# A decoder layer's self-attention: projection parts in odd steps, other work in even steps, and a DMA that adds the fourth tile of three quads

## The chip, the core and the metric

The kernel runs on one core of a Trainium2 chip. The metric is the device time of one execution in microseconds (us). A core has TensorE (PE, matmuls; PEld is its weight load), VectorE (DVE), ScalarE (ACT), GpSimd (POOL) and SyncE (SP, which here only issues DMAs). Each runs its own instruction stream, and the streams wait for one another through semaphores.

## What is computed

A decoder layer on x of 2 x 2048 x 512: self-attention of 16 heads, a layer norm of the sum, cross-attention over 77 context rows, a layer norm, a mixture of 8 experts, a layer norm. The change concerns the self-attention alone:

```python
qkv = x @ qkv_w + qkv_b
q, k, v = ...                                   # 16 heads of 32
attn = softmax(einsum('bnhd,bmhd->bhnm', q, k) * scale)
out = einsum('bhnm,bmhd->bnhd', attn, v) @ proj_w + proj_b
```

## The kernel before

A unit is one batch with four heads (their 4 x 32 features fill 128 partitions); there are 8 units. A unit's 2048 queries are cut into four chunks of 512, so there are 32 chunks (g = 0 to 31). A chunk goes over the 2048 keys in 16 steps (kt) of 128 keys. In each step TensorE makes four scores, one per head (line 706, keys x queries, 128 x 512), in three banks in rotation, and ScalarE takes their exponentials (line 472) into one of four tiles of prob, by kt % 4.

The softmax's shift is the row maximum. It is found ahead: between the scores of chunk g TensorE also makes the 64 maximum passes (line 631) of chunk g + 1, four per step and three steps early, so that the passes of chunk g + 2 begin in step 13 (T - EARLY). They go to three banks (mx) in rotation; VectorE reduces each (line 517), and a pass waits for the reduction three passes before it. After step 12 VectorE takes the maxima over the parts (line 522), negates them (line 526) and makes a low part (line 528); TensorE transposes these in step 13 into the bank misc (line 644), VectorE copies them out in step 14 (line 535), and SyncE issues four DMAs that put the rows below the queries (line 318), at the end of its chunk's list. The next chunk's scores wait for them.

In each even step, after the second score, TensorE runs a burst: it multiplies the values with the two tiles before (line 652). Row sums (the softmax's denominators) go through GpSimd: the tiles of a chunk form four quads, and GpSimd adds tiles 1, 2 and 3 of a quad to its sum, two heads at a time (add_step, line 273, six additions per quad). TensorE sums a quad over the keys (line 660) into misc, quads 0 and 1 in step 15, quads 2 and 3 in steps 1 and 2 of the next chunk. ScalarE copies the sums out in step 2 (line 452), VectorE inverts them in four pieces in steps 3 and 4 (line 542), GpSimd multiplies the values' sums by them (divide, line 279) and SyncE stores the result (line 325). ScalarE may write a prob tile again once GpSimd's addition of it is done.

The queries, keys and values of the units are projected in between. A job (OPS, JOBS) is one 512-wide block of q, k or v in four parts, a part being one matmul of 512 columns (q and k, line 623) or four of 128 (v, line 619) into misc. Up to three jobs stand in a chunk, their parts at the steps of PARTS_AT: a step's first of two parts stands after its second score, the last part at the step's end. In the step after a job's last part (LEAVE_AT) VectorE takes it out of misc: for q and k a rounded high part (line 509) and a low part (line 511), for v one addition (line 498). The first part of the next job waits for that. SyncE, which goes through a fixed list by kt, then issues twelve DMAs of 64 KB per q or k job (move_stack, line 245) that stack high and low parts for the scores, and where a block of x has had its last user the load of the next one (line 312, 1 MB). In step 13 TensorE waits for the stacked queries that chunk g + 2 reads (line 743): in the third and fourth chunk of a unit these come from the chunk's own second job. Chunks 28 to 31 belong to the last unit; only two of its jobs are left there.

The lines that set the order of SyncE's and VectorE's lists around the change:

```python
SUMS_AT, DENS_AT, DIVIDE_AT, STORE_AT = 0, 2, (1, 1), 10
INVERT_AT = ((3, 1), (3, 3), (4, 1), (4, 3))
PARTS_AT = ((3, 3, 4, 5), (6, 7, 7, 8), (9, 10, 11, 11))
LEAVE_AT = {(job.chunk, job.place[-1] + 1): i for i, job in enumerate(JOBS) if job.place}
```

Of the kernel before, what the change touches and what calls it, by code (L numbers as in the profile page):

```python
# [13 lines left out]
P = 128  # L14
# [61 lines left out]
def self_attention(nc, z, keep, block, x, xT_dram, qkv_w, qkv_b, attnT_dram, rows_dram):  # L76
# [13 lines left out]
    LEAD = EARLY * PER_STEP  # L90
    MOVES = 3 * HG
# [4 lines left out]
    QUADS, ADDS = T // 4, 6  # L96
# [5 lines left out]
    SUMS_AT, DENS_AT, DIVIDE_AT, STORE_AT = 0, 2, (1, 1), 10  # L102
    INVERT_AT = ((3, 1), (3, 3), (4, 1), (4, 3))
# [8 lines left out]
    PARTS_AT = ((3, 3, 4, 5), (6, 7, 7, 8), (9, 10, 11, 11))  # L112
# [33 lines left out]
    def stacked_by(i):  # L146

        return 16 * sum(MOVES // 2 if other.place is None else MOVES for other in JOBS[:i + 1]
                        if (other.what, other.n) == (JOBS[i].what, JOBS[i].n))

# [61 lines left out]
    quad_ready, den_mm, recip_ready = s.sem("quad_ready"), s.sem("den_mm"), s.sem("recip_ready")  # L212
# [37 lines left out]
    def _(pool):  # L250
# [9 lines left out]
        def add_step(g, i, k):  # L260


            d = g * QUADS + i
            if k == 1:

                after(pool, den_mm, d - QUADS + 1)
            for half in range(2):
                heads = slice(2 * half, 2 * half + 2)
                pool.wait_ge(prob_ready, (g * T + 4 * i + k) * HG + 2 * half + 2)
                if k > 1:  # L270
                    pool.wait_ge(quad_ready, d * ADDS + 2 * (k - 1) - 1 + half)
                so_far = prob[:, 0, heads, :] if k == 1 else quad_sum[:, i, heads, :]
                pool.tensor_tensor(quad_sum[:, i, heads, :], so_far, prob[:, k, heads, :], ALU.add).then_inc(quad_ready, 1)  # L273
# [24 lines left out]
    def _(sp):  # L298
# [50 lines left out]
        for g in range(LAST):  # L349
            for kt in range(T):  # L350
                if kt == STORE_AT and g > 0:
                    store(g - 1)
                    empty_slots(g - 4)
                if (g, kt) not in LEAVE_AT:
                    continue
# [13 lines left out]
            shift_rows(g + 1)  # L369
# [26 lines left out]
    def _(act):  # L396
# [31 lines left out]

        for chunk in range(NQ):
            load_rows(chunk)  # L430
# [23 lines left out]
        def exponentials(g, fill=None):  # L454
            for kt in range(T):
                step = g * T + kt
                for j in range(HG):
# [26 lines left out]
    def _(dve):  # L484
# [5 lines left out]
        def leave_psum(i):  # L490
# [12 lines left out]
            if job.place is not None:  # L503
                before = SPLITS[order - 2]
                if JOBS[before].place is None:
                    stacked_first(dve, JOBS[before].what, JOBS[before].n)
                else:
                    dve.wait_ge(stacked[JOBS[before].what, JOBS[before].n], stacked_by(before))
                dve.tensor_scalar(hilo[:, order % 2, 0, :], bank[:, :], bias, None, ALU.add).then_inc(hi_ready, 1)
# [4 lines left out]
        def reduce_max(n, m):  # L514
            dve.wait_ge(max_mm, n + 1)
            q, j, k = m // (HG * KQ), m // KQ % HG, m % KQ
            dve.reduce_max(part_max[:, q, j, k:k + 1], mx[n % 3][:, :], AX_X).then_inc(max_read, 1)  # L517
# [36 lines left out]
        for m in range(2):  # L554
            reduce_max(NMAX + m, m)
        leave_shift(0)
        for m in range(2, LEAD):
            reduce_max(NMAX + m, m)

        for g in range(LAST):  # L560
            for kt in range(T):
                for i in range(PER_STEP):
                    n = (g + 1) * NMAX + LEAD + kt * PER_STEP + i
                    if n < CHUNKS * NMAX:
                        reduce_max(n, n % NMAX)
                    if i == 0 and kt == T - EARLY + 1 and g + 1 < CHUNKS:
# [3 lines left out]
                    if (kt, i) in INVERT_AT and g > 0:  # L570
                        invert(g - 1, INVERT_AT.index((kt, i)))
# [9 lines left out]
    def _(pe):  # L581
# [11 lines left out]
        def project_part(i, part):  # L593
# [5 lines left out]
            if part == 0:  # L599
# [9 lines left out]
                if not first and JOBS[i - 1].chunk != job.chunk:  # L609
                    if job.chunk > 0:  # L610
                        pe.wait_ge(dens_ready, job.chunk)
                    else:
                        pe.wait_ge(shiftT_ready, 1)
# [13 lines left out]
        def max_pass(n, m, g):  # L627

            after(pe, max_read, n - 2)
            q, j, k = m // (HG * KQ), m // KQ % HG, m % KQ  # L630
            pe.matmul(mx[n % 3][:, :], q_stack[g % Q_SLOTS][0:QK, j, q * P:(q + 1) * P], k_stack[g // NQ % 2][0:QK, j, k * BANK:(k + 1) * BANK],  # L631
                      start=True, stop=True).then_inc(max_mm, 1)

        def transpose_shift(g):

            pe.wait_ge(shift_ready, g + 1)
            before = [i for (chunk, kt), i in LEAVE_AT.items() if chunk == g - 1]
            if g > 1:
                pe.wait_ge(dens_ready, g - 1)
            if before:  # L640
                i = before[-1]
                pe.wait_ge(v_ready if JOBS[i].what == "v" else hilo_ready, left_psum(i))
            for q in range(TQ):
                last = pe.transpose(misc[0:2 * HG, q * P:(q + 1) * P],
# [11 lines left out]
        def row_sums(d):  # L656

            pe.wait_ge(quad_ready, (d + 1) * ADDS)
# [26 lines left out]
        def burst(g, kt):  # L685
# [12 lines left out]
            for i in OWN_SUMS_AT.get(kt, ()):  # L698
                if i == 0:
                    pe.wait_ge(shiftT_ready, g + 2)  # L700
# [27 lines left out]
        for m in range(LEAD):  # L728
            if m == 2:
# [5 lines left out]
        def chunk(g):  # L735
            pe.wait_ge(shift_in, (g + 1) * 16 * HG)
            for kt in range(T):
# [7 lines left out]
                for i in range(HG):  # L745
                    n = (g + 1) * NMAX + LEAD + kt * PER_STEP + i
                    if n < CHUNKS * NMAX:
# [1459 lines left out]
```

## Time and profile before

| | |
|---|---|
| runs, median (lowest to highest) | 3611.71 us (3609.11 to 3613.97), 3 runs |
| profiled execution, its own time | 3609.78 us |
| its span, first to last instruction | 3608.1 us |
| TensorE busy over the span | 3360.5 us, 93% |
| VectorE busy | 2530.3 us, 70% |
| GpSimd busy | 1996.3 us, 55% |
| ScalarE busy | 1640.8 us, 45% |
| mean granted clock of TensorE | 0.97 |
| stretch of chunks 0 to 31 | about 110 to 2135 us of the span |

The span is one execution on the core; the rest of the execution's time lies around it. Busy shares are of the whole span, of which the self-attention's chunks are the part from about 110 us; the cross-attention and the experts follow. "Granted clock" is TensorE's clock as the records give it, 1.00 being 2.4 GHz and 0.50 being 1.2. Matmuls are pipelined, so that their busy times overlap: where this document prices one, it goes from one start to the next. In the rows, an engine's idle time before an instruction stands in brackets with what ended it.

### The profile page before, as it was taken

The numbers are of one execution on the slowest core, as the hardware profiler recorded it, in microseconds if no ns is written. First come the engines' busy times: TensorE is split into PE (matmuls) and PEld (weight loads), VectorE is DVE, ScalarE is ACT, GpSimd is POOL, SyncE is SP. The second block draws the span as 40 slices with busy tenths as digits, with TensorE's granted clock in tenths as the row PEclk, the third lists the DMA queues.
The fourth block names the chain that finished last, engine by engine and source line by source line (L and its number), as shares of the span: only waits on it lengthen the run. The fifth ranks groups of instructions, "written<-read, shape, count | busy, mean of one in ns | idle before, by whom it ended". The sixth has DMA issues, their size and how long they took to land. (4 is left out here: it accounts for less than half of the span.)

```text
span 3608.1 us, 50073 instructions
## 1 busy us (share of the span) xinstructions
PE 3360.5 (93%) x18021; PEld 2253.7 (62%) x18021; DVE 2530.3 (70%) x4512; ACT 1640.8 (45%) x3043; POOL 1996.3 (55%) x1008
## 2 busy tenths in 40 slices
PE   7999999999999999999999887999859899999996
PEld 5555555555555555554554445887749789898885
DVE  5777777777777777777777745888734765566666
ACT  2455555555555555555555553444312332233332
POOL 2698898998898898898898930011110101110112
PEclk9999999999999999999999988999979999999998
DMA  6312222322313313223220032132132333323332
GB/s 218 111 56 67 71 75 65 94 68 62 110 39 85 87 51 105 55 63 94 62 71 13 16 107 66 56 113 94 47 126 71 131 105 109 110 95 107 127 124 96
DMA packets 190276, 308.47 MB, mean 85 GB/s; under 512 B 25513, under 2 KB 72233, under 8 KB 190010
## 3 DMA queue, kind: packets, MB, share of 16 engines
q1 hardware_dynamic: 166970, 243.82, 22.7%
q0 software_dynamic: 14592, 44.32, 3.6%
q10 hardware_dynamic: 8448, 16.78, 1.3%
q8 instruction: 167, 2.74, 0.3%
q14 instruction: 99, 0.81, 0.1%
HBM read 195.66 MB, written 61.33 MB: 71 GB/s over the span
## 5 line engine op out<-in xcount | busy, mean ns | idle before, releaser
L517 DVE TENSOR_REDUCE sa_part_max<-sa_mx 128x1 f32<-128x512 f32 x2048 | 1288.2, 680 | 487.1 <-PE sa_mx L631 483.8
L472 ACT ACTIVATE sa_prob<-sa_sc 128x512 f32<-128x512 f32 x2017 | 1072.6, 600 | 804.4 <-PE sa_sc L706 755.5
L273 POOL TENSOR_TENSOR sa_quad_sum<-sa_quad_sum,sa_prob 128x1024 f32<-128x1024 f32 x500 | 1175.5, 2381 | 8.1 <-ACT sa_prob L472 7.5
L273 POOL TENSOR_TENSOR sa_quad_sum<-sa_prob 128x1024 f32<-128x1024 f32 x250 | 588.7, 2375 | 225.4 <-ACT sa_prob L472 223.3
L2072 PE MATMUL ex_h<-ex_xT,ex_w 128*128 128x384 f32 (+2 forms) x2688 | 464.0, 328 | 52.2 <-issue 24.1
L631 PE MATMUL sa_mx<-sa_k_even,sa_q_stack 96*128 96x512 f32 x1024 | 492.1, 484 | 9.3 <-DMA sa_q_stack<-sa_shiftT 3.1
L2072 PEld LDWEIGHTS ex_h<-ex_xT,ex_w 128*128 128x128 f32 x2688 | 445.9, 195 | 64.5 <-issue 31.8
L631 PE MATMUL sa_mx<-sa_k_odd,sa_q_stack 96*128 96x512 f32 x1024 | 481.1, 470 | 1.8 <-DVE sa_part_max L517 1.3
L2083 PE MATMUL ex_acc<-ex_w,ex_hT 128*128 128x512 f32 x1719 | 415.6, 392 | 1.5 <-DVE ex_hT L2011 1.3
L706 PE MATMUL sa_sc<-sa_q_stack,sa_k_even 98*128 98x512 f32 x1024 | 407.3, 398 | 0.0
L706 PE MATMUL sa_sc<-sa_q_stack,sa_k_odd 98*128 98x512 f32 x993 | 393.9, 400 | 0.4 <-ACT sa_prob L472 0.4
L2083 PEld LDWEIGHTS ex_acc<-ex_w,ex_hT 128*128 128x128 f32 x1719 | 317.1, 188 | 65.2 <-issue 3.8
L631 PEld LDWEIGHTS sa_mx<-sa_k_odd,sa_q_stack 96*128 96x128 f32 x1024 | 193.9, 189 | 220.8 <-DVE sa_part_max L517 121.5
L631 PEld LDWEIGHTS sa_mx<-sa_k_even,sa_q_stack 96*128 96x128 f32 x1024 | 195.3, 191 | 215.6 <-DVE sa_part_max L517 97.5
L1845 POOL DMA_DIRECT2D ex_xg<-rows x48 | 26.4, 555 | 529.4 <-PE ex_h L2051 529.1
L1916 ACT ACTIVATE ex_h<-ex_h,ex_b 128x384 f32<-128x384 f32 x256 | 145.2, 580 | 380.3 <-PE ex_h L2072 380.3
L652 PE MATMUL sa_pv<-sa_prob,sa_v_odd 128*32 128x512 f32 x2048 | 251.2, 606 | 0.6 <-ACT sa_prob L472 0.5
L652 PE MATMUL sa_pv<-sa_prob,sa_v_even 128*32 128x512 f32 x2048 | 246.2, 598 | 0.0
L706 PEld LDWEIGHTS sa_sc<-sa_q_stack,sa_k_even 98*128 98x128 f32 x1024 | 195.7, 191 | 57.2 <-ACT sa_prob L472 29.8
L706 PEld LDWEIGHTS sa_sc<-sa_q_stack,sa_k_odd 98*128 98x128 f32 x993 | 189.6, 192 | 62.8 <-ACT sa_prob L472 34.7
L1098 POOL TENSOR_TENSOR ca_rstd<-ca_var_eps,ca_minus_half 128x8 f32<-128x8 f32 x16 | 26.5, 1654 | 324.1 <-DVE ca_var_eps L1166 324.1
L2009 DVE CAST ex_hT<-ex_h 128x384 fp32r<-128x384 f32 x256 | 94.3, 368 | 144.6 <-ACT ex_h L1916 144.1
(229 smaller groups left out, 3768.1 us busy)
## 6 DMA issues: line engine op xcount, KB each, us to landing
ex_w_in<-in_L_ffn_w_dram SPq DMA_DIRECT2D x130, 512.0 KB, 4.5
sa_xT<-xT SPq DMA_DIRECT2D x57, 1024.0 KB, 5.6
sa_q_stack<-sa_hilo SPq DMA_DIRECT2D x372, 64.0 KB, 2.0
rows<-sa_empty SPq DMA_DIRECT2D x48, 257.0 KB, 4.8
ex_rows<-rows POOLq DMA_DIRECT2D x8, 1542.0 KB, 8.0
sa_k_odd<-sa_hilo SPq DMA_DIRECT2D x192, 64.0 KB, 2.0
ex_xg<-rows POOLq DMA_DIRECT2D x48, 256.0 KB, 3.0
sa_k_even<-sa_hilo SPq DMA_DIRECT2D x168, 64.0 KB, 2.0
```

What stands on the lines that cost most here:

```text
L273: pool.tensor_tensor(quad_sum[:, i, heads, :], so_far, prob[:, k, heads, :], ALU.add).then_inc(quad_ready, 1)
L472: act.activation(prob[:, kt % 4, j, :], score_bank(n)[:, :], ACT.Exp, scale=SCALE).then_inc(prob_ready, 1)
L517: dve.reduce_max(part_max[:, q, j, k:k + 1], mx[n % 3][:, :], AX_X).then_inc(max_read, 1)
L631: pe.matmul(mx[n % 3][:, :], q_stack[g % Q_SLOTS][0:QK, j, q * P:(q + 1) * P], k_stack[g // NQ % 2][0:QK, j, k * BANK:(k + 1) * BANK], sta ...
L652: last = pe.matmul(pv[D * j:D * (j + 1), :], v[buf][:, kt, D * j:D * (j + 1)], prob[:, kt % 4, j, :], start=(kt == 0), stop=(kt == T - 1))
L706: pe.matmul(score_bank(n)[:, :], k_stack[g // NQ % 2][0:AUG, j, kt * P:(kt + 1) * P], q_stack[g % Q_SLOTS][0:AUG, j, :], start=True, stop= ...
L1098: pool.tensor_tensor(rstd[:, which, :, :], var_eps[:, which, :, :], minus_half[:, :, :], ALU.pow).then_inc(rstd_ready, 1)
L1845: pool.dma_start(xg[:, t, :], a.rows[row:row + P, 0:C]).then_inc(gathered, 16)
L1916: act.activation(h[:, j % 2, half * HALF:(half + 1) * HALF], h_bank[half][:, 0:HALF], ACT.Gelu, bias=b1[:, step:step + 1]).then_inc(h_read ...
L2009: dve.tensor_copy(hT[:, j % 2, 0, cols], h[:, j % 2, cols]).then_inc(hT_hi, 1)
L2072: last = pe.matmul(h_bank[half][:, 0:slots], w1[:, i % 2, pw, k, :], xT[:, e % 2, px, k, half * HALF:half * HALF + slots], start=(part == ...
L2083: last = pe.matmul(acc[t][:, :], hT[:, i % 2, ph, t * P:(t + 1) * P], w2[:, i % 2, pw, :], start=(i == 0 and part == 0), stop=(i == STEPS ...
```

## The change

The projection parts of a chunk's jobs move to steps 3 to 13, two in each odd step, and the jobs' leaving to steps 6, 10 and 14. Of a q or k job ScalarE makes the high part (ACT.Identity with the bias), ahead of its second exponential of that step; VectorE keeps the low part and the values. The four inverses go to steps 4 and 8, two at a time, the division to the third quad's second addition, the store to step 13. The shift's transposes go into one of the three mx banks, as a turn of their rotation (turn_of, shift_turn, turn_left), its copy to step 13, its four DMAs in SyncE's list to step 14, ahead of that step's stack moves. In the first three quads of a chunk GpSimd adds tiles 1 and 2 itself and issues one DMA of 1 MB, SBUF to SBUF, that adds tile 3 to the sum; ScalarE (for the tile) and TensorE (for the row sums) wait for its landing (fourth_in). Cut to its core:

```diff
@@ -88,19 +88,22 @@
+    SHIFT_TURN = 3
...
-    QUADS, ADDS = T // 4, 6
+    QUADS = T // 4
+    ADDS = (4, 4, 4, 6)
+    HIGH_HEAD = 1
...
-    SUMS_AT, DENS_AT, DIVIDE_AT, STORE_AT = 0, 2, (1, 1), 10
-    INVERT_AT = ((3, 1), (3, 3), (4, 1), (4, 3))
+    SUMS_AT, DENS_AT, DIVIDE_AT, STORE_AT = 0, 2, (2, 2), 13
+    INVERT_AT = (4, 4, 8, 8)
...
-    PARTS_AT = ((3, 3, 4, 5), (6, 7, 7, 8), (9, 10, 11, 11))
+    PARTS_AT = ((3, 3, 5, 5), (7, 7, 9, 9), (11, 11, 13, 13))
...
+    def turn_of(n):
+        return n + max((n - SHIFT_TURN) // NMAX, 0)
+    def shift_turn(g):
+        return (g + 1) * NMAX + SHIFT_TURN + g
+    def turn_left(engine, turn):
...
+    def adds_until(d):
+        return d // QUADS * sum(ADDS) + sum(ADDS[:d % QUADS])
+    def fourths_until(d):
+        return d - d // QUADS
@@ -264,11 +297,17 @@ (gpsimd, add_step)
+            if k == 3 and i < QUADS - 1:
+                pool.wait_ge(prob_ready, (g * T + 4 * i + k + 1) * HG)
+                pool.wait_ge(quad_ready, adds_until(d + 1))
+                pool.dma_start(quad_sum[:, i, :, :], prob[:, k, :, :], accum_op=ALU.add).then_inc(fourth_in, 16)
+                return
@@ -351,6 +390,8 @@ (sync, loop over kt)
+                if kt == T - EARLY + 1:
+                    shift_rows(g + 1)
...
-            shift_rows(g + 1)
@@ -426,6 +466,18 @@ (scalar)
+        def leave_high_part(i):
+            job, order = JOBS[i], SPLITS.index(i)
+            act.wait_ge(proj_mm, i + 1)
+            before = SPLITS[order - 2]
+            if JOBS[before].place is None:
+                stacked_first(act, JOBS[before].what, JOBS[before].n)
+            else:
+                act.wait_ge(stacked[JOBS[before].what, JOBS[before].n], stacked_by(before))
+            bias = qkb[:, 0 if job.what == "q" else 1, job.unit % G:job.unit % G + 1]
+            act.activation(hilo[:, order % 2, 0, :], misc[:, :], ACT.Identity, bias=bias).then_inc(hi_ready, 1)
@@ -462,13 +514,19 @@ (scalar, exponentials)
+                    if j == HIGH_HEAD and (g, kt) in LEAVE_AT and JOBS[LEAVE_AT[g, kt]].what != "v":
+                        leave_high_part(LEAVE_AT[g, kt])
...
-                        act.wait_ge(quad_ready, (step // 4 - 1) * ADDS + 2 * max(kt % 4 - 1, 0) + j // 2 + 1)
+                        d, k, half = step // 4 - 1, max(kt % 4, 1), j // 2
+                        if k < 3 or d % QUADS == QUADS - 1:
+                            act.wait_ge(quad_ready, adds_until(d) + 2 * (k - 1) + half + 1)
+                        elif j == 0:
+                            act.wait_ge(fourth_in, 16 * fourths_until(d + 1))
@@ -500,13 +558,6 @@ (vector, leave_psum)
-            if job.place is not None:
...
-                dve.tensor_scalar(hilo[:, order % 2, 0, :], bank[:, :], bias, None, ALU.add).then_inc(hi_ready, 1)
@@ -532,7 +583,7 @@ (vector, leave_shift)
-            dve.tensor_copy(shiftT[:, :], misc[0:2 * HG, :]).then_inc(shiftT_ready, 1)
+            dve.tensor_copy(shiftT[:, :], mx[shift_turn(g) % 3][0:2 * HG, :]).then_inc(shiftT_ready, 1)
@@ -551,24 +602,23 @@ (vector, loop over kt and i)
-                    if i == 0 and kt == T - EARLY + 1 and g + 1 < CHUNKS:
+                    if i == 2 and kt == T - EARLY:
                         leave_shift(g + 1)
...
-                    if (kt, i) in INVERT_AT and g > 0:
-                        invert(g - 1, INVERT_AT.index((kt, i)))
+                    for q in range(TQ):
+                        if i == 1 and kt == INVERT_AT[q] and g > 0:
+                            invert(g - 1, q)
@@ -626,22 +674,17 @@ (tensor)
-            after(pe, max_read, n - 2)
+            turn_left(pe, turn_of(n) - 3)
...
-                last = pe.transpose(misc[0:2 * HG, q * P:(q + 1) * P],
+                last = pe.transpose(mx[shift_turn(g) % 3][0:2 * HG, q * P:(q + 1) * P],
@@ -655,7 +698,9 @@ (tensor, row_sums)
-            pe.wait_ge(quad_ready, (d + 1) * ADDS)
+            pe.wait_ge(quad_ready, adds_until(d + 1))
+            if d % QUADS < QUADS - 1:
+                pe.wait_ge(fourth_in, 16 * fourths_until(d + 1))
```

Left out are the new waits' bookkeeping (turn_left counts the reductions and copies that have freed a bank), the same shift turn in the start-up, TensorE's waits for misc that go with the shift's move, and its wait ahead of the row sums of step 15, which is now for the chunk's last job.

## Rows read from the trace of the kernel before

**Rows 1.** Windows: chunks 1 to 27, then 28 to 30; busy us of each engine, clock, DMA
```profile
172.80:1893.30 1720.50, 1685.30 (x9205) 921.24 (x9204) 1291.17 (x2079) 950.65 (x1783) 1552.98 (x676) 1.00 0.26 72
1893.30:2086.50 193.20, 171.05 (x881) 83.11 (x880) 147.48 (x209) 104.79 (x199) 172.52 (x77) 0.92 0.05 13
```

**Rows 2.** Windows: pairs of steps 0/1 to 14/15 of chunk 14; PE PEld DVE ACT POOL
```profile
1000.84:1007.82 6.98, 6.98 (x42) 3.45 (x40) 4.96 (x9) 4.72 (x11) 6.28 (x4) 1.00 0.00 0
1007.82:1016.21 8.39, 8.39 (x45) 4.39 (x44) 6.08 (x10) 5.31 (x11) 8.39 (x5) 1.00 0.01 3
1016.21:1023.83 7.62, 7.62 (x38) 4.08 (x37) 7.43 (x12) 4.25 (x8) 5.52 (x3) 1.00 0.00 0
1023.83:1032.20 8.37, 8.37 (x40) 4.49 (x38) 6.60 (x11) 4.34 (x8) 8.37 (x5) 1.00 0.24 56
1032.20:1041.26 9.06, 7.79 (x44) 4.56 (x42) 6.47 (x10) 4.24 (x8) 8.36 (x5) 1.00 0.18 40
1041.26:1049.76 8.50, 8.50 (x58) 6.07 (x57) 5.15 (x8) 4.34 (x8) 8.32 (x4) 1.00 0.50 131
1049.76:1056.55 6.79, 6.78 (x37) 3.39 (x36) 5.33 (x11) 3.80 (x8) 4.31 (x3) 1.00 0.96 221
1056.55:1064.56 8.01, 8.01 (x49) 3.63 (x48) 5.81 (x11) 4.20 (x9) 8.01 (x4) 1.00 0.02 5
```

**Rows 3.** Timeline of PE in steps 7 and 9 of chunk 14: start, us, what
```profile
1029.06 0.40 PE L706 MATMUL sa_sc<-sa_q_stack,sa_k_odd 98*128 98x512 f32 x1
...
1030.40 0.39 PE L706 MATMUL sa_sc<-sa_q_stack,sa_k_odd 98*128 98x512 f32 x1
...
1030.86 0.40 PE L706 MATMUL sa_sc<-sa_q_stack,sa_k_odd 98*128 98x512 f32 x1
...
1040.06 1.13 PE L619 MATMUL sa_misc<-sa_wkv,sa_xT 128*128 128x128 f32 x8 [1.27 <-DVE sa_hilo L511]
```

**Rows 4.** Waits from 172 to 1893 us: us in total, times, longest
```profile
PE sa_misc L619 <- DVE sa_hilo L511: 26.7, 21, 1.3
...
PE sa_misc L623 <- DVE sa_hilo L511: 7.6, 6, 1.3
```

**Rows 5.** The tile sa_shift, whole run: ns min/median/max, first and last start
```profile
L526 DVE TENSOR_SCALAR sa_shift<-sa_top x32: 174/176/7105, 99.7 to 2069.4; 128x16 fp32r<-128x16 f32 x32
```

**Rows 6.** Timeline of VectorE and of GpSimd, chunk 28
```profile
1939.68 7.10 DVE L526 TENSOR_SCALAR sa_shift<-sa_top 128x16 fp32r<-128x16 f32 x1
...
1944.42 2.33 POOL L273 TENSOR_TENSOR sa_quad_sum<-sa_prob 128x1024 f32<-128x1024 f32 x1
```

**Rows 7.** Timeline of VectorE and of GpSimd, chunk 14
```profile
1054.58 0.18 DVE L526 TENSOR_SCALAR sa_shift<-sa_top 128x16 fp32r<-128x16 f32 x1
...
1054.88 3.07 DVE L517 TENSOR_REDUCE sa_part_max<-sa_mx 128x1 f32<-128x512 f32 x5
...
1055.38 4.71 POOL L273 TENSOR_TENSOR sa_quad_sum<-sa_prob 128x1024 f32<-128x1024 f32 x2 [2.48 <-ACT sa_prob L472]
```

**Rows 8.** Timeline of SyncE's DMA issues, chunk 14
```profile
1040.00 7.74 SPq L245 DMA_DIRECT2D sa_q_stack<-sa_hilo  x12
```

**Rows 9.** The tile sa_hilo from 300 to 1700 us: landing of its DMAs
```profile
DMA to landing us min/median/max: 1.9/2.0/4.1
```

**Rows 10.** The page's DMA issues: KB each, median us to landing
```profile
sa_xT<-xT SPq DMA_DIRECT2D x57, 1024.0 KB, 5.6
...
ex_rows<-rows POOLq DMA_DIRECT2D x8, 1542.0 KB, 8.0
...
ex_xg<-rows POOLq DMA_DIRECT2D x48, 256.0 KB, 3.0
```

**Rows 11.** Line 427, ScalarE's high parts in the first stage: ns min/median/max
```profile
L427 ACT ACTIVATE sa_hilo<-sa_misc,sa_qkb x3: 687/687/687, 28.6 to 63.2; 128x512 fp32r<-128x512 f32 x3
```

**Rows 12.** The tile sa_recip, whole run: inverse and division
```profile
L542 DVE RECIPROCAL sa_recip<-sa_recip x128: 894/941/954, 186.3 to 2140.5; 128x128 f32<-128x128 f32 x128
...
L279 POOL TENSOR_TENSOR sa_recip<-sa_sums,sa_recip x32: 1260/1272/1292, 199.3 to 2141.6; 128x512 f32<-128x512 f32 x32
```

More of the change, by code:

```diff
@@ L149, in stacked_by, with maximum_at @@
                         if (other.what, other.n) == (JOBS[i].what, JOBS[i].n))
+    def turn_of(n):
[3 more added lines that the diff above has]
+    def turn_left(engine, turn):
+        users = turn // (NMAX + 1) + 2
+        shifts = [g for g in range(users) if shift_turn(g) == turn]
+        if shifts:
+            engine.wait_ge(shiftT_ready, shifts[0] + 1)
+        elif turn >= 0:
+            engine.wait_ge(max_read, min(turn - sum(1 for g in range(users) if shift_turn(g) < turn) + 1, CHUNKS * NMAX))
+    def maximum_at(g, kt, i):
+        n = (g + 1) * NMAX + LEAD + kt * PER_STEP + i
+        return [n] if n < CHUNKS * NMAX else []
+    def adds_until(d):
+        return d // QUADS * sum(ADDS) + sum(ADDS[:d % QUADS])
+    def fourths_until(d):
+        return d - d // QUADS
     def job_of(unit, what, n):
@@ L270, in add_step @@
                 if k > 1:
-                    pool.wait_ge(quad_ready, d * ADDS + 2 * (k - 1) - 1 + half)
+                    pool.wait_ge(quad_ready, adds_until(d) + 2 * (k - 2) + half + 1)
                 so_far = prob[:, 0, heads, :] if k == 1 else quad_sum[:, i, heads, :]
@@ L502, in leave_psum @@
             bias = qkb[:, 0 if job.what == "q" else 1, job.unit % G:job.unit % G + 1]
-            if job.place is not None:
[L504 to L508, printed above, removed]
-                dve.tensor_scalar(hilo[:, order % 2, 0, :], bank[:, :], bias, None, ALU.add).then_inc(hi_ready, 1)
             dve.wait_ge(hi_ready, order + 1)
@@ L553, in _ @@
         make_shift(0)
[L554 to L557, printed above, removed]
+        for m in range(LEAD):
+            if m == SHIFT_TURN:
+                leave_shift(0)
             reduce_max(NMAX + m, m)
@@ L561, in _ @@
             for kt in range(T):
-                for i in range(PER_STEP):
-                    n = (g + 1) * NMAX + LEAD + kt * PER_STEP + i
-                    if n < CHUNKS * NMAX:
+                for i in range(HG):
+                    for n in maximum_at(g, kt, i):
                         reduce_max(n, n % NMAX)
-                    if i == 0 and kt == T - EARLY + 1 and g + 1 < CHUNKS:
+                    if i == 2 and kt == T - EARLY:
                         leave_shift(g + 1)
@@ L627, in max_pass @@
         def max_pass(n, m, g):
-            after(pe, max_read, n - 2)
+            turn_left(pe, turn_of(n) - 3)
             q, j, k = m // (HG * KQ), m // KQ % HG, m % KQ
-            pe.matmul(mx[n % 3][:, :], q_stack[g % Q_SLOTS][0:QK, j, q * P:(q + 1) * P], k_stack[g // NQ % 2][0:QK, j, k * BANK:(k + 1) * BANK],
+            pe.matmul(mx[turn_of(n) % 3][:, :], q_stack[g % Q_SLOTS][0:QK, j, q * P:(q + 1) * P], k_stack[g // NQ % 2][0:QK, j, k * BANK:(k + 1) * BANK],
                       start=True, stop=True).then_inc(max_mm, 1)
@@ L636, in transpose_shift @@
             pe.wait_ge(shift_ready, g + 1)
[L637 to L642, printed above, removed]
+            turn_left(pe, shift_turn(g) - 3)
             for q in range(TQ):
-                last = pe.transpose(misc[0:2 * HG, q * P:(q + 1) * P],
+                last = pe.transpose(mx[shift_turn(g) % 3][0:2 * HG, q * P:(q + 1) * P],
                                     shift[:, q, :, :].bitcast(F32).rearrange("p j a -> p (j a)"), ident[:, :])
@@ L698, in burst @@
             for i in OWN_SUMS_AT.get(kt, ()):
-                if i == 0:
-                    pe.wait_ge(shiftT_ready, g + 2)
+                before = [job for (chunk, step), job in LEAVE_AT.items() if chunk == g]
+                if i == 0 and before:
+                    pe.wait_ge(v_ready if JOBS[before[-1]].what == "v" else hilo_ready, left_psum(before[-1]))
                 row_sums(g * QUADS + i)
@@ L728, in _ @@
         for m in range(LEAD):
-            if m == 2:
+            if m == SHIFT_TURN:
                 transpose_shift(0)
@@ L745, in chunk @@
                 for i in range(HG):
-                    n = (g + 1) * NMAX + LEAD + kt * PER_STEP + i
-                    if n < CHUNKS * NMAX:
+                    for n in maximum_at(g, kt, i):
                         max_pass(n, n % NMAX, n // NMAX)
```

6 lines of the change are left out of this document (2 added, 4 removed).

## Prediction

> **What bounds the kernel now.** I read the stretches first. Chunks 1 to 27 of the self-attention take 1720.5 us, 63.7 each, with TensorE busy for 1685 of them at a granted clock of 1.00 (its full 2.4 GHz) while VectorE is busy for 1291 and ScalarE for 951; chunks 28 to 30, which project next to nothing, take longer still, 193.2 us or 64.4 each, at a mean clock of 0.92 [rows 1]. What follows is worth the 28 full chunks, so I cut chunk 14 into its eight pairs of steps, from the first score matmul of an even step to the next [rows 2]. A pair's fixed load is 8 maximum passes, 8 scores and one burst of value matmuls. To see what else each pair holds, the timeline of TensorE prices a projection part: from one score to the next (line 706) is 0.46 us (1030.40 to 1030.86), and where a part stands between them, as in step 7's middle, 1.34 (1029.06 to 1030.40), so a part is 0.88 us [rows 3]. Taking the parts off by the positions in the code: pair 6/7 holds three, 8.37 - 2.63 = 5.7; pair 4/5 two, 7.62 - 1.75 = 5.9; pair 10/11 three, 8.50 - 2.63 = 5.9. Two pairs stand out. Pair 8/9 has two parts and 9.06 us, 7.3 without them: its step 9 holds the wait of TensorE for VectorE's low part (1.27 us, row 1040.06), which the table of waits has 27 times in 27 chunks (21 and 6), 34.3 us [rows 3, 4]. Pair 12/13 has no part, and 6.79 us less about 0.6 for the four shift transposes is 6.2: there TensorE outruns VectorE, whose 8 maxima of some 0.61 us (3.07 for five [rows 7]) fill 4.9 of the pair and leave it late for the rest. So in the full chunks TensorE's own work is the bound, with a loss of about 1.3 us in one place and of some 0.4 in pairs without parts.
>
> Late chunks lose elsewhere. In chunk 28 VectorE's small negation of the maxima, 0.18 us in the median, takes 7.10 us; it starts at 1939.68, and ends at 1946.78, when GpSimd's run of additions ends (1944.42 + 2.33) [rows 5, 6]. In chunk 14 the same instruction stands at 1054.58, inside GpSimd's gap of 2.48 us that ends at 1055.38, and takes 0.18 [rows 7]. It costs nothing only as long as GpSimd is idle then.
>
> **The change, part by part.**
> *Projections in odd steps.* Twelve parts as before, now two in each of steps 3 to 13. Pairs 0/1 and 2/3 keep their content: 6.98 and 8.39. Pairs 4/5, 6/7, 8/9 and 10/11 hold two parts each: 5.7 + 1.75 = 7.5 at the least, 7.62 as measured in pair 4/5; I take 7.55, four times 30.2. Pair 12/13 gains two parts: 8.1 (5.7 + 1.75 + 0.6) to 8.5 (6.79 + 1.75); I take 8.25, as the parts give VectorE the time it lacked. Pair 14/15 loses the copy of the shift to step 13 but gets the third job's leaving: 7.8 to 8.01, I take 7.95. Sum 61.8 against 63.72, a gain of 1.95 us (1.3 to 2.45); over chunks 0 to 27, 55 us (37 to 69). The wait in step 9 is part of it: the next job's first part now comes a whole step after the leaving, some 5 us behind it.
>
> *VectorE's other work.* High parts leave VectorE for ScalarE, two per chunk in the mean, 0.69 us each by the first stage's rows [rows 11]. ScalarE is busy for 55% of the stretch [rows 1], and in an even step it then waits for the burst anyway: nothing. The high part waits for the stack moves of two jobs before, at least 8 steps old; behind it stand the exponentials of its own step only. Inverses go two together into steps 4 and 8, 1.88 us [rows 12]; VectorE is idle for 2.0 of the 6.98 us of pair 0/1 [rows 2], most of it under the burst, and an odd step with two parts (3.6) gives it 1.1 over its four maxima: nothing. The shift's transposes move from the projection bank to the maximum banks and take one turn of their rotation; a maximum pass three turns later waits for the copy, done by then by my order of the step.
>
> *Queues moved past.* SyncE issues the four shift rows at step 14, ahead of the third job's moves; the copy comes about a step earlier, so they land well ahead of the next chunk. The second job's twelve moves begin a step later, in step 10. In chunks 2 and 3 of a unit, 14 of the 28, they carry the queries that the maxima of step 13 read. Twelve issues take 7.74 us and the last lands 2.0 later [rows 8, 9]; begun 2.5 us into step 10 they end at 12.2, and step 13 begins at 3.95 + 3.6 + 3.95 = 11.5. With the overlap of issue and landing I take 0.5 us of waiting, 7 us in all; between nothing and 2.6 us each (36) if the last landing takes the 4.1 of the slowest.
>
> *A DMA adds the fourth tile.* GpSimd drops 6 of 24 additions per chunk, 14 us, for three issues of 0.5 to 0.9 (issues of 256 and 1542 KB). No accumulating DMA is in the trace. From the two plain transfers on GpSimd's queue, 3.0 us for 256 KB and 8.0 for 1542 [rows 10], a plain 1 MB would take 6.0; an addition reads its destination too, so 6.0 is one end, 10.0 with the 4.0 of data doubled, 14.0 with them taken three times the other. I take 10, the case of two reads. The tile is complete when step 4i+4 begins and ScalarE overwrites it from step 4i+7: 7.55 + 3.95 = 11.5 us, and 1.3 more by the three score banks. For the third quad GpSimd finishes its own additions and a division of 1.27 first [rows 12], which leaves 11.2 of 12.5. So 10 is hidden, with little to spare; two row sums wait for it much later. The Trainium skill (Collectives: The Full Stack, section on why ReduceScatter is half of AllGather) says that an inline addition costs through its second source read, which halves the rate; by it the transfer is 10.0 as well, and the sum stays.
>
> *Late chunks.* GpSimd then falls idle ahead of step 13, and the 7 us stalls of three chunks go: three times 6.9 us. The mean clock of 0.92 over 193 us is 31 us at the lower level (1.2 GHz), 10 per chunk, 7 of them idle in the stall, so 3 us of work run at half speed and 1.5 are lost: 25 in all, an estimate from rows 1 and 6. Without parts these steps are short, GpSimd is done with quad 2 barely 0.3 us before the negation comes, and the third landing comes close: I give 4 back, 21 (0 to 25).
>
> **Sum.** 55 + 21 - 7 = 69 us off the profiled execution's 3609.8: 3541. That execution is 1.9 under the median of the runs, so 3543.
>
> **Rivals.**
> *The addition lands too late (0.17).* Slower. From about 13.0 us (mean of 13.3, 13.3 and 12.5) each of 93 transfers stalls ScalarE, and TensorE with it; the gain is gone at 13.8. At the upper bound of 14 the stalls are 0.7 + 0.7 + 1.5 per chunk, 90 us: 3633; every further us costs 93. For it: the inputs' 1 MB loads (5.6 us [rows 10]) and two stores fall beside it on the same DMA engines. Against: each tile has three steps.
>
> *The negation meets GpSimd in every chunk (0.08).* If GpSimd runs 2.7 us later than I order it, the gap before step 13 closes and VectorE waits for an addition of 2.4 us, 2.2 of it on TensorE's path: 28 times, 62 us, 3605, no change. Against: 14 us of additions a chunk go. The Trainium skill (SBUF — State Buffer, Who interferes with whom) says that the second of two such instructions blocks until the first is finished; by it the rows of chunk 28 agree, and this would be the result wherever they meet.
>
> *The moved queries are late (0.11).* The last moves share the DMA engines with the third addition and wait 2.5 us in 14 chunks: 28 more, 3571. For it: landings of 4.1 occur [rows 9].
>
> *The wait returns (0.03).* If ScalarE's high part comes over 2 us late, first parts wait again, twice a chunk: 2 x 1.3 x 28 = 73, 3616.
>
> **How the numbers follow.** The forecast has 0.61. The range, 3512 to 3606, takes in its bounds (69 + 25 with no wait below, and 6 more if pairs 0/1 and 14/15, whose fixed load is 0.3 above the others', give 0.1 each), the late queries and the met negation: 0.61 + 0.11 + 0.08 = 0.80. Below the median by over 0.2% (7 us, about what a measurement of this kernel can tell): 0.61 + 0.11 + 0.02 of the met negation = 0.74. Within it: its other 0.06 and 0.01 of the returning wait. Slower: 0.17 + 0.02 = 0.19.
>
> **What would show it.** Right: a chunk of about 61.8 us, pairs 4 to 11 near 7.55, no wait of a part for a low part, the negation at 0.18 in all 32 chunks, the accumulating transfers landing under 12 us. Wrong: ScalarE waiting for a DMA into the quad sums at steps 7, 11 and 15, a negation of over 1 us, or TensorE waiting at step 13 for stacked queries.

## The result, and the profile after

The kernel after takes 3644.26 us (median of 4 runs, 3637.87 to 3652.52) against 3612.45 (3609.11 to 3613.97) before: a ratio of 1.0087, 95% interval 1.0066 to 1.0108. It is slower by 0.9%, where 3543 was forecast. The profiled execution took 3644.66, of which 3642.8 are its span.

The page of the kernel after, in its parts on the span, the engines, the queue of GpSimd's DMAs (packets, MB, share), and the issues (count, KB each, median us to landing):

```profile
span 3642.8 us, 49911 instructions
PE 3370.0 (93%) x18021; PEld 2290.7 (63%) x18021; DVE 2479.6 (68%) x4454; ACT 1671.6 (46%) x3101; POOL 1636.9 (45%) x914
...
q0 software_dynamic: 28128, 142.89, 17.2%
...
sa_quad_sum<-sa_prob POOLq DMA_DIRECT2D x94, 1024.0 KB, 8.1
```

GpSimd lost 359 us of work (1996.3 to 1636.9) and VectorE 51, as the change meant, and the core became slower. Where, the stretches say. Windows of the kernel after (start and end, span, then busy us and instructions of PE, PEld, DVE, ACT and POOL, granted clock, DMA share, GB/s): chunks 1 to 27, the four chunks 12 to 15 of one unit, and chunks 28 to 30.

```profile
170.33:1944.13 1773.80, 1694.07 (x9206) 957.62 (x9204) 1268.81 (x2026) 978.29 (x1837) 1245.03 (x595) 0.97 0.49 118
```
```profile
894.43:955.82 61.39, 61.39 (x318) 32.42 (x317) 46.97 (x76) 36.72 (x71) 46.11 (x23) 1.00 0.59 146
955.82:1017.36 61.54, 61.54 (x341) 34.48 (x340) 46.80 (x76) 36.12 (x70) 46.08 (x23) 1.00 0.57 139
1017.36:1087.56 70.20, 64.47 (x341) 36.63 (x340) 47.18 (x76) 36.37 (x70) 46.11 (x23) 0.93 0.40 95
1087.56:1156.88 69.32, 63.78 (x366) 38.15 (x364) 47.02 (x76) 35.78 (x69) 46.15 (x23) 0.95 0.43 106
1944.13:2110.19 166.06, 163.99 (x881) 79.58 (x879) 125.97 (x207) 106.75 (x201) 135.10 (x66) 1.00 0.34 72
```

Against [rows 1], chunks 1 to 27 take 53.3 us more (1720.50) and chunks 28 to 30 27.1 less (193.20). But the full chunks are of two kinds. The first two of a unit (chunks 12 and 13 here) take 61.4 and 61.5, without one idle us of TensorE, a little under the 61.8 forecast. The third and fourth take about 8 more; over all units, from first score to first score, the four places have means of 61.2, 61.6, 69.3 and 69.9. The pairs of steps of chunk 14, a third chunk, to lay beside [rows 2] (the same columns):

```profile
1017.36:1024.34 6.98, 6.98 (x41) 3.45 (x40) 4.96 (x9) 4.73 (x10) 5.11 (x3) 1.00 0.00 1
1024.34:1032.72 8.38, 8.38 (x45) 4.39 (x44) 5.53 (x9) 5.32 (x11) 8.07 (x4) 1.00 0.01 2
1032.72:1040.23 7.51, 7.51 (x37) 4.13 (x36) 6.73 (x10) 4.24 (x8) 2.73 (x2) 1.00 0.69 140
1040.23:1047.74 7.51, 7.51 (x37) 4.13 (x36) 5.81 (x9) 4.81 (x9) 7.51 (x4) 1.00 0.22 52
1047.74:1055.25 7.51, 7.51 (x37) 4.13 (x36) 6.73 (x10) 4.24 (x8) 2.74 (x3) 1.00 0.90 180
1055.25:1062.83 7.58, 7.58 (x49) 5.17 (x48) 5.81 (x9) 4.82 (x9) 7.58 (x5) 1.00 0.30 67
1062.83:1079.69 16.86, 11.13 (x53) 7.50 (x52) 6.50 (x12) 4.56 (x8) 4.57 (x4) 0.70 0.55 133
1079.69:1087.54 7.85, 7.85 (x49) 3.72 (x48) 5.09 (x9) 3.63 (x7) 7.76 (x4) 1.00 0.39 136
```

Seven pairs are where they were put. The eighth, 12/13, takes 16.86 instead of 8.25, at a clock of 0.70. The waits from 172 to 1893 us name the cause (waiting engine, tile and line, what it waited for: us in total, times, longest):

```profile
PEld sa_mx L679 <- DMA sa_q_stack<-sa_hilo: 80.0, 13, 6.6
PE sa_mx L679 <- DMA sa_q_stack<-sa_hilo: 74.3, 13, 6.2
```

The maximum passes of step 13 wait for the stacked queries, 13 times in that stretch (the fourteenth lies behind it), 5.7 us on TensorE in the mean. That the projection parts no longer wait for a low part (27 times, 34.3 us in [rows 4]) is as forecast: that row is gone. Chunk 14 in detail; the timelines of GpSimd, of SyncE's DMA issues and of TensorE, and the landings of the three moves issued from 1063.69 on, the last of twelve:

```profile
1063.98 0.83 POOL L304 DMA_DIRECT2D sa_quad_sum<-sa_prob  x1
```
```profile
1062.42 3.12 SPq L278 DMA_DIRECT2D sa_q_stack<-sa_hilo  x5
1065.59 1.42 SPq L364 DMA_DIRECT2D attnT<-sa_recip  x1
```
```profile
1066.30 0.40 PE L752 MATMUL sa_sc<-sa_q_stack,sa_k_odd 98*128 98x512 f32 x1
1072.43 0.80 PE L679 MATMUL sa_mx<-sa_k_even,sa_q_stack 96*128 96x512 f32 x1 [5.73 <-DMA sa_q_stack<-sa_hilo]
1073.03 0.63 PE L752 MATMUL sa_sc<-sa_q_stack,sa_k_odd 98*128 98x512 f32 x1
```
```profile
DMA to landing us min/median/max: 2.0/5.2/7.4
```

GpSimd issues the third addition at 1063.98; it lands 8.2 us later, at 1072.2. SyncE issues its last two moves 0.3 and 1.0 us behind it (at 1064.32 and 1064.96). They land after 5.2 and 7.4 instead of 2.0: the last with the addition, and TensorE starts at 1072.43. TensorE has stood idle since 1066.7. Its granted clock is 0.50 (1.2 GHz) from 1068.3 to 1078.6, inside the stall and 6 us beyond: the score behind it takes 0.63 instead of 0.40. All 14 such chunks have a stretch at 0.50, of 6.8 or 10.2 us.

The negation is what it was to become in all 32 chunks, beside [rows 5]; the landings of the DMAs on the quad sums follow. The view counts four stores of the start-up with them, to which the 4.1 belongs; the 94 additions alone land after 6.9 to 10.6 us, 8.1 in the median:

```profile
L577 DVE TENSOR_SCALAR sa_shift<-sa_top x32: 175/176/177, 99.0 to 2102.2; 128x16 fp32r<-128x16 f32 x32
```
```profile
DMA to landing us min/median/max: 4.1/8.0/10.6
```

One more loss of the same family stands in chunk 31. There the next stage's loads run beside the additions, the slowest of which lands after 10.6 us, and ScalarE waits 7.1 us before it may write a tile again; step 8 takes 9.43 us instead of 2.98. The row is from the waits between 2113 and 2150 us:

```profile
ACT sa_prob L530 <- DMA sa_quad_sum<-sa_prob: 7.1, 1, 7.1
```

### The profile page after: what moved, and what is told of

It reads as the page before. It is cut to its first block and busy times, and to the rows that moved or that the text cites. A ratio compares the mean times of both kernels' runs of the same rounds, so it can differ in the third digit from the quotient of the medians.

```text
span 3642.8 us, 49911 instructions
## 1 busy us (share of the span) xinstructions
PE 3370.0 (93%) x18021; PEld 2290.7 (63%) x18021; DVE 2479.6 (68%) x4454; ACT 1671.6 (46%) x3101; POOL 1636.9 (45%) x914
## 5 line engine op out<-in xcount | busy, mean ns | idle before, releaser
L312 POOL TENSOR_TENSOR sa_quad_sum<-sa_quad_sum,sa_prob 128x1024 f32<-128x1024 f32 x312 | 736.2, 2379 | 2.2 <-ACT sa_prob L530 0.4
L1956 ACT ACTIVATE ex_w<-ex_w_in 128x512 fp32r<-128x512 f32 x128 | 80.6, 630 | 217.2 <-PE ex_acc L2128 217.2
```

Source lines behind the costliest of these rows:

```text
L1956: act.activation(w2[:, j % 2, 0, :], w2_in[:, j // 2, j % 2, :], ACT.Copy).then_inc(w2_hi, 1)
```

## The experiments

The theory: the moves' delay behind the third addition is the whole loss, and everything else of the forecast holds. The rivals: the addition as such (reading its destination) or GpSimd's issue hurts; the steps' new order itself is worse; or the gain never was in the steps.

**add_waits: the third addition goes behind the moves.** In chunks that move queries GpSimd waits for their landing before it issues the third quad's DMA.

```diff
@@ add_step
+                moved = LEAVE_AT.get((g, 10))
+                if i == 2 and moved is not None and JOBS[moved].what == "q":
+                    pool.wait_ge(stacked["q", JOBS[moved].n], stacked_by(moved))
                 pool.dma_start(quad_sum[:, i, :, :], prob[:, k, :, :], accum_op=ALU.add).then_inc(fourth_in, 16)
```

> The changed kernel, but in the third and fourth chunk of a unit GpSimd issues the third adding DMA only after the twelve query moves have landed. Theory A (the last two moves are issued just behind the 1 MB addition and land only with it, 7.4 us instead of 2.0): the wait of TensorE at step 13 goes, 14 chunks fall from about 69.5 to 61.7 us, the time to about 3535 (3522 to 3550). The addition lands some 3 us later and may just touch ScalarE's step 15. Rival B (the moves are late because they begin one step later, whatever the addition does): nothing changes, 3644.

Measured: 3544.96 us (3542.28 to 3549.03), ratio 0.9818 (0.9801 to 0.9834). Windows of chunks 1 to 27, of the third chunk 14, and of chunks 28 to 30; then the waits for moved queries from 172 to 1893 us:

```profile
169.26:1843.69 1674.43, 1664.99 (x9205) 933.94 (x9204) 1265.73 (x2026) 976.67 (x1837) 1244.54 (x595) 1.00 0.51 125
```
```profile
974.14:1036.09 61.95, 61.60 (x341) 34.47 (x340) 46.93 (x76) 36.33 (x70) 46.11 (x23) 1.00 0.46 107
...
1843.69:2009.73 166.04, 163.95 (x880) 79.59 (x879) 125.94 (x207) 106.73 (x201) 135.05 (x66) 1.00 0.34 72
```
```profile
POOL sa_quad_sum L307 <- DMA sa_q_stack<-sa_hilo: 30.4, 7, 4.7
...
PEld sa_mx L682 <- DMA sa_q_stack<-sa_hilo: 15.5, 14, 1.9
...
PE sa_mx L682 <- DMA sa_q_stack<-sa_hilo: 9.0, 9, 1.5
```

Three lines turn a loss of 0.9% into a gain of 1.8%, and only the time of one issue differs: TensorE's wait falls from 74 us to 9, the clock is 1.00, and of GpSimd's own wait of 30 us no row shows a cost. The addition goes out in step 13 and is still hidden; chunk 31, which moves no queries, keeps its long step (9.93 us). As expected: the theory holds. What is left of the moves' wait is 1.1 us a chunk on the weight loads.

**no_dma: no DMA adds; GpSimd does all 24 additions again.** The steps' new order alone. The counts and waits that go with it are left out here.

```diff
-    ADDS = (4, 4, 4, 6)
+    ADDS = (6, 6, 6, 6)
+    BY_DMA = 0
...
-            if k == 3 and i < QUADS - 1:
+            if k == 3 and i < BY_DMA:
```

> The changed kernel with all 24 additions of a chunk on GpSimd, no adding DMA. Theory A: no wait for query moves over 1 us at step 13; they land 2 us after their issue. But GpSimd has 58 us of work in a chunk of 61.7, so its gap ahead of step 13 closes and VectorE's negation of the maxima meets the additions: stalls of 2 us or more in all chunks, the time between 3540 and 3750. Rival B: the waits of 6 us for the query moves at step 13 stay in 14 chunks.

Measured: 3623.87 us (3615.82 to 3632.38, 10 runs), ratio 1.0035 (1.0023 to 1.0047). The waits of 6 us for the moves are gone, though TensorE still waits 0.2 to 2.8 us in eight chunks, where none over 1 us was expected. But another wait stands in their place: the negation's row, over the whole run, and the waits from 172 to 1893 us.

```profile
L578 DVE TENSOR_SCALAR sa_shift<-sa_top x32: 174/2184/7248, 97.8 to 2078.9; 128x16 fp32r<-128x16 f32 x32
```
```profile
PEld sa_mx L688 <- DVE sa_shift L580: 48.5, 18, 3.6
...
PEld sa_mx L680 <- DMA sa_q_stack<-sa_hilo: 14.8, 14, 3.2
```

With the fourth tile back on GpSimd its additions reach into step 13, and the negation waits for them: about 3.3 us in the first two chunks of a unit, 1.0 in the others (2 or more were expected in all), up to 7.2 in the late ones. The 28 full chunks take 62.4 us more than with add_waits (1796.4 against 1733.9). So the DMA is worth its place, though not for the 14 us of additions as such: it clears GpSimd before the negation.

**two_quads: the DMA only for quads 0 and 1.** Only the addition that meets the moves goes back to GpSimd; the other lines are those of no_dma.

```diff
-    ADDS = (4, 4, 4, 6)
+    ADDS = (4, 4, 6, 6)
+    BY_DMA = 2
```

> The changed kernel with the adding DMA for the first two quads only; GpSimd adds the third quad's fourth tile itself. Theory A: no large transfer is ahead of the query moves at step 12, they land in 2 us and the 6 us waits at step 13 go. GpSimd's additions and division of the third quad then end some 2 us into step 13, after the negation comes (0.9 us in), so that it takes 1 to 3 us in the chunks 0 to 27 and the time is 3560 to 3610. If GpSimd's additions did not hold the negation up, 3545.

Measured: 3642.28 us (3627.93 to 3649.49), ratio 1.0089 (1.0073 to 1.0105). The same two views:

```profile
L578 DVE TENSOR_SCALAR sa_shift<-sa_top x32: 176/2187/5834, 97.5 to 2075.3; 128x16 fp32r<-128x16 f32 x32
```
```profile
PEld sa_mx L688 <- DVE sa_shift L580: 48.8, 19, 3.5
...
PEld sa_mx L680 <- DMA sa_q_stack<-sa_hilo: 14.0, 14, 1.8
```

The moves are as expected: with two additions a chunk left, the longest wait for them is 1.8 us. The time was expected too low, by over 30 us: a stalled negation costs more than its own length where the clock falls behind it (0.97 over chunk 12), and the late chunks stay at 189 us. Over the 28 full chunks this kernel takes 1793.2 us, hardly less than no_dma (1796.4), so there two additions by DMA of three are worth little more than none, and only the third frees GpSimd in time. In chunk 31 it loses besides what no_dma does not: ScalarE waits 6.0 us for an addition, and step 8 takes 8.38 us instead of 2.98. Why the runs of this kernel lie as far apart as 3628 and 3649 was not tried; the rows are of the one at 3628.

**plain_copy: every addition by DMA as a plain copy.** The kernel after with a copy in its place; the first three tiles of three quads are lost from their sums.

```diff
-                pool.dma_start(quad_sum[:, i, :, :], prob[:, k, :, :], accum_op=ALU.add).then_inc(fourth_in, 16)
+                pool.dma_start(quad_sum[:, i, :, :], prob[:, k, :, :]).then_inc(fourth_in, 16)
```

> The changed kernel, its DMA of 1 MB copies the fourth tile over the quad's sum instead of adding to it, so the first three tiles' share of three quads is lost from the row sums. Theory A (what counts is that a large transfer is ahead of the moves): it lands in about 6 us instead of 8.1, the last two moves in about 5, and the wait at step 13 shrinks from 6 to 3 or 4 us: about 3600. Rival C (what counts is the addition): the moves land in 2 us and no wait is left: 3535.

Measured: 3612.49 us, one run. The page's row of the 94 transfers (count, KB each, median us to landing), and the waits from 172 to 1893 us:

```profile
sa_quad_sum<-sa_prob POOLq DMA_DIRECT2D x94, 1024.0 KB, 5.3
```
```profile
PEld sa_mx L679 <- DMA sa_q_stack<-sa_hilo: 50.3, 13, 5.4
PE sa_mx L679 <- DMA sa_q_stack<-sa_hilo: 44.6, 13, 5.0
```

The wait is there for a plain copy as well, shorter by 2.3 us a time (44.6 for 74.3 us) where the transfer lands 2.8 us sooner (5.3 for 8.1). So a megabyte ahead is enough for a wait of 3.4 us; the adding counts by the time for which it makes the transfer longer.

**add_halves: two DMAs of 512 KB for each addition.** The waits for fourth_in count 32 for 16.

```diff
-                pool.dma_start(quad_sum[:, i, :, :], prob[:, k, :, :], accum_op=ALU.add).then_inc(fourth_in, 16)
+                for half in range(2):
+                    heads = slice(2 * half, 2 * half + 2)
+                    pool.dma_start(quad_sum[:, i, heads, :], prob[:, k, heads, :], accum_op=ALU.add).then_inc(fourth_in, 16)
```

> The changed kernel, each adding DMA cut in two of 512 KB, two heads each (rows of 4 KB instead of 8). If a small transfer is held up by the size of the large one's rows, the last query moves land in 5 us or less and the wait at step 13 is 4 us or less: about 3610. If it is held up by the bytes ahead, as theory A has it, the last move sees the same 1 MB: landings near 7, the waits near 6, the time within 15 us of 3644.

Measured: 3632.59 us, one run. The moves' waits shrink by about a quarter, to 62.8 us on the weight loads (80.0) and 57.1 on TensorE (74.3), 4.4 us in the mean; the longest is still 6.8 on the weight loads. The time is 12 us below the kernel after, in one run. That lies between the two cases expected: the time is the one of the bytes ahead, the mean wait is nearer to the 4 us of the smaller rows. So smaller pieces help a little, and the run does not decide between the two.

**dma_alone: the kernel before, with the DMA additions and nothing else.** The waits for fourth_in go with it as in the change.

```diff
@@ add_step of the kernel before
+            if k == 3 and i < QUADS - 1:
+                pool.wait_ge(prob_ready, (g * T + 4 * i + k + 1) * HG)
+                pool.wait_ge(quad_ready, adds_until(d + 1))
+                pool.dma_start(quad_sum[:, i, :, :], prob[:, k, :, :], accum_op=ALU.add).then_inc(fourth_in, 16)
+                return
```

> The kernel before with nothing but the fourth tile of three quads added by a DMA. Theory A: the second job's moves are over before the third addition begins, so no wait at step 13 of the chunks 0 to 27, which stay at 63.7 us; the three 7 us negations of the late chunks go: about 3588 (3575 to 3612). If the adding DMA costs something of itself wherever it runs (rival B'): waits of ScalarE for it, and the time above 3612.

Measured: 3618.24 us (3616.14 to 3626.53, 10 runs), ratio 1.0024 (1.0015 to 1.0034): a miss, 30 us above what was expected. The negation is at 174 to 177 ns in all 32 chunks and the late chunks take 167.4 us, as expected. But the full chunks lose, where they were expected to stay: chunks 1 to 27 take 1740.6 us for 1720.5, and most of it falls on the first two of a unit (65.8 and 64.6 us for 63.5 and 63.7). Two new waits stand in the table. ScalarE's for the additions, which with the time above 3612 was to be the sign of rival B', is found in all four places of a unit, but TensorE's weight loads of the scores wait hardly longer for ScalarE than before (51.1 us for 49.6). The wait for the shift rows reaches TensorE (14.3 us for 0.3), nearly all of it at the end of a unit's first chunk. The waits from 172 to 1893 us:

```profile
ACT sa_prob L491 <- DMA sa_quad_sum<-sa_prob: 20.4, 18, 2.4
...
PEld sa_mx L650 <- DMA sa_q_stack<-sa_shiftT: 18.3, 11, 3.7
```

Chunk 12, the timelines of GpSimd's and SyncE's issues:

```profile
932.46 0.87 POOL L280 DMA_DIRECT2D sa_quad_sum<-sa_prob  x1 [1.43 <-ACT sa_prob L491]
```
```profile
933.20 0.45 SPq L327 DMA_DIRECT2D sa_xT<-xT  x1
935.40 10.33 SPq L254 DMA_DIRECT2D sa_k_even<-sa_hilo  x12
945.77 2.48 SPq L333 DMA_DIRECT2D sa_q_stack<-sa_shiftT  x4
```

The addition lands after 9.6 us and the load of x after 11.3, at 944.5; the first of the twelve moves lands after 9.2, at 944.6. The moves take 10.33 us to issue instead of 7.74 [rows 8], and the four shift rows behind them come late for the next chunk. It is the same collision in another place, here with the load of x as well, and with other victims: the wait that reaches TensorE is again for what SyncE issues behind the large transfers. It makes up 11 of the 20 us lost in chunks 1 to 27; the rest is not accounted for, so that this run does not exclude rival B'.

**q_first: in a unit's fourth chunk the queries are the first job.**

```diff
-           Op("v", 0, 1, 3, 6), Op("q", 1, 1, 3, 7), Op("v", 1, 1, 3, 7)]
+           Op("q", 1, 1, 3, 7), Op("v", 0, 1, 3, 6), Op("v", 1, 1, 3, 7)]
```

> The changed kernel, but in the fourth chunk of a unit the query job is the first of the three instead of the second, so its moves go out in steps 6 to 8. Theory A (it is those moves, and their place beside the third addition): the wait at step 13 goes in these 7 chunks and stays in the 7 third chunks: 7 x 8.5 = 60 us less, about 3584. Rival B (a large addition beside SyncE's list costs as much whatever is moved): 3644.

Measured: 3590.5 us (3586.24 to 3595.38), ratio 0.9944 (0.9928 to 0.9959). Chunks 14 and 15:

```profile
994.15:1063.21 69.06, 63.37 (x342) 35.96 (x341) 47.19 (x76) 36.35 (x70) 46.10 (x23) 0.95 0.41 96
1063.21:1124.91 61.70, 61.70 (x366) 36.58 (x364) 46.66 (x76) 35.54 (x69) 46.03 (x23) 1.00 0.48 116
```

The fourth chunk loses its stall with the addition left where it was; the third keeps it. In the fourth no move stands beside the third addition any more. That the meeting itself is harmless where nobody waits for the moves shows in the kernel after: in chunk 13 the last two of twelve moves, of keys, stand 0.1 and 0.7 us behind the addition and land after 2.1 and 7.1 us, and the chunk takes 61.5.

**add_waits_last: GpSimd's wait, and chunk 31's quads added by GpSimd.** With the edit of add_waits, this condition, and the counts and waits to match:

```diff
-            if k == 3 and i < QUADS - 1:
+            if k == 3 and i < QUADS - 1 and g < LAST:
```

> As the kernel whose third addition waits for the query moves, and in the last chunk, where the next stage's loads fill the DMA engines, GpSimd adds the fourth tile of its one quad itself. Theory A: step 8 of the last chunk falls from 9.9 us to 3, the time from 3545 to about 3538 (3531 to 3543), below the kernel before by 2%. Rival: the loads stall that step in another way (a later tile of the same chunk), and nothing is gained, 3545.

Measured: 3539.15 us (3531.43 to 3542.53), ratio 0.9791 (0.9777 to 0.9805); chunk 31's long step is 2.98 us again, as expected.

**all_three: the same with the edit of q_first.**

> The version with GpSimd's wait and the last quad by GpSimd, and beside it the query job of a unit's fourth chunk taken as that chunk's first job, so that only the third chunk still needs the wait. If the moved queries are the only thing that holds a fourth chunk up, its mean goes from 62.7 to 61.6 us, the third chunk stays at 62.6, TensorE's waits for stacked queries are halved (some 8 us on the weight loads instead of 16), and the time is 7 x 1.1 = 8 us below the 3539 of that version: 3531 (3525 to 3538). If the rest of a fourth chunk comes from the third addition's landing or from the fourth prob tile, the mean stays near 62.7 and the time near 3539.

Measured: 3533.1 us (3523.79 to 3539.89, 5 runs), ratio 0.9778 (0.9759 to 0.9797). The fourth chunks take 61.6 us in the mean, the third 62.5. The waits from 172 to 1893 us:

```profile
PEld sa_mx L682 <- DMA sa_q_stack<-sa_hilo: 7.4, 7, 2.1
```

As expected. Of all the versions this one has the lowest median, 2.2% below the kernel before; its interval overlaps that of add_waits_last.

## Why the prediction was wrong, step by step

*The stretch and its bound* were read rightly. The pairs came at 7.51, 7.51, 7.51 and 7.58 where 7.55 was taken, and 14/15 at 7.85 for 7.95; in an undisturbed chunk (13) pair 12/13 takes 8.16 for 8.25. High parts on ScalarE, inverses by twos and the shift in the maximum banks cost TensorE nothing, as costed.

*The late chunks* gained 27.1 us for 21 taken, above the range of 0 to 25. No part of the 4 us given back was needed, and the clock, 1.00 for 0.92, came back fully.

*The failed step* is "Queues moved past": 0.5 us of waiting per third and fourth chunk, "between nothing and 2.6 us each (36) if the last landing takes the 4.1 of the slowest". It was 5.7 us of TensorE's wait with some 2.4 more, most of it at the lower clock behind it (step 13, from its first score on, takes 6.05 us in the mean of the 14 chunks, 4.25 in chunk 13), 8.1 us a chunk (69.6 in the mean of both places against the 61.5 of chunks 12 and 13) and 14 x 8.1 = 113 us. The place was right, also in the rival "The moved queries are late"; its price of 2.5 us was a third of the true one. The bound was read from the wrong number. In [rows 9] 4.1 looks like the worst that a move can do. But two moves of that stretch land after 4.1 us, and neither meets what the change brings. One, issued at 1620.88, has only smaller transfers beside it, a store of 256 KB and two transfers of 257 KB, issued 0.6 to 1.8 us behind it. The other stands behind a load of x: the timeline of SyncE's issues in chunk 12, then the landings of the load (issued at 922.60) and of the first of the twelve moves.

```profile
922.60 0.45 SPq L312 DMA_DIRECT2D sa_xT<-xT  x1
925.35 7.49 SPq L245 DMA_DIRECT2D sa_k_even<-sa_hilo  x12
```
```profile
DMA to landing us min/median/max: 6.9/6.9/6.9
```
```profile
DMA to landing us min/median/max: 4.1/4.1/4.1
```

The load of 1 MB landed at 929.5, and the move issued 2.75 us behind it at 929.4. This 4.1 was no property of the move but the rest of the megabyte ahead of it (there on the same queue). In chunks 1 to 27 of the kernel before, no load of x is issued less than 2.6 us ahead of a move; in chunk 14 of the kernel after the addition is issued 0.3 us ahead. So 4.1 was no bound for that. Read so, the prediction's own figures give the stall: an addition issued 1.3 us into step 12 (the 12.5 less the 11.2) that lands 10 us later, and maxima due at step 12 + 3.95, make 10 + 1.3 - 3.95 = 7.35 us, before any clock. With the 1.15, 8.2 and 3.9 of chunk 14 it is 5.5, for 5.7 measured.

*The third addition's other effects* were sized on the safe side: 8.1 us to land where 10 was taken, and ScalarE waits for no addition in the full chunks. In chunks 29 and 30 it waits 1.3 us each, and in chunk 31 step 8 lost 6.4 us: the prediction did not look at what the next stage loads beside it. The 13.3 us of its first rival do not come out of its own 11.5 + 1.3 = 12.8; with 8.1 measured nothing hangs on it.

*The sum.* Forecast against the profiled execution: 48 for the full chunks (55 - 7) and 21 for the late ones. With the stall taken away by add_waits, chunks 1 to 27 give 46.1 us (1720.50 to 1674.43; 27 x 1.95 - 7 = 45.7 forecast) and the late ones 27.2; chunk 31 and what lies around take some 7 back, and the time is 3545 for the 3543 forecast. That it comes so near is in part luck: in chunks 1 to 27 the steps gave 2.2 us each for 1.95 and the waits left over cost 13 for 7, and the late chunks' 6 us more and chunk 31's loss cancel as well. In the kernel after, chunks 1 to 27 lose 53.3: the stalls' 113 us, less 27 times the 2.2 gained.

*The rivals.* "The negation meets GpSimd in every chunk" did not happen, but no_dma shows its price: 62.4 us over the full chunks, for 62 worked out. The sum agrees by luck: 2.2 us were taken for every chunk, and measured against add_waits are 4.2, 4.1, 0.1 and 0.5 by place in the unit. The Trainium skill (SBUF — State Buffer, Who interferes with whom) says that the second of two such instructions blocks until the first has finished; the stalls of 1.0 us agree, each with the rest of one addition. Those of 3.3 and 7.2 us are longer than any one addition (2.4), so that VectorE there waited through more than one of a run: in chunk 12 of no_dma from 924.6 to 928.0, over two additions that end at 925.7 and 928.0. "The addition lands too late" fell, except in chunk 31. "The wait returns" fell: no part waits for a low part.

## What to carry to other kernels

Before a large transfer is put on a free queue, list the small transfers that will be issued within its landing time, whatever their queue, and ask who waits for them; cost each at the rest of the large one, not at its own row (here up to 7.7 us for 2.0). A slowest landing is a bound only after one has looked at what was in flight beside it. And where a transfer is hidden with time to spare, let it wait for the urgent ones: the wait is on the engine that has nothing to lose.

## What had not been expected of the hardware

In chunk 14 the 64 KB moves that SyncE issues 0.3 and 1.0 us behind a 1 MB transfer from GpSimd land in 5.2 and 7.4 us instead of 2.0, the last with the megabyte; with the pieces halved the same two take 4.4 and 6.3. The Trainium skill (DMA: Bandwidth & Descriptors, Queues, rings and completion order) says that each DMA engine takes turns between its queues packet by packet. By that a move would have to share the engines with the addition, not to wait for its end. The trace's records of single packets agree that they take turns, though not equal ones. The addition's 128 packets of 8 KB start from 1065.4 to 1070.9 and take 0.64 us each in the median. The first 32 packets of 2 KB behind it, as many as one move has, start among them, from 1066.75 to 1068.5; then none of SyncE's 2 KB packets starts until 1070.0, by when 112 of the 128 have started. Once started, such a packet takes 0.10 us, no longer than those of the moves ahead of the addition (0.15 in the median). So by these records the small packets wait to be started and are not moved more slowly. What sets the length of a turn stays open.

SyncE's issues slow down as well beside the addition: 1.42 us for the one issue of the store (line 364) in chunk 14 of the kernel after, 0.58 in the same place with add_waits, where the addition goes out later.

An adding transfer of 1 MB from SBUF to SBUF lands in 8.1 us in the median, a plain one in 5.3. Less the 2.0 of a small move that is 6.1 against 3.3, a ratio of 1.8; from the fastest of either kind (6.9 and 4.3) it is 2.1. The Trainium skill (Collectives: The Full Stack, why ReduceScatter is half of AllGather) has the rate halved by the second source read, and the runs agree roughly.

A stall of TensorE of some 6 us is not its whole price: in the 14 chunks its clock falls to 0.50 within the stall and stays there for 3.3 to 6.5 us beyond it. That cost 2.4 us more in chunk 14 (step 13 takes 6.7 us instead of 4.25) and 1.8 in the mean.
